# A graph network on one core: one scatter per node row in the first norm, edge rows kept by place, last stage unrolled

## The chip, the cores and the metric

The kernel runs on one core of one Trainium2 chip (trn2). The metric is device time in microseconds (us) of one launch. The engines are TensorE (PE, with its weight loads shown apart as PEld), VectorE (DVE), ScalarE (ACT), GpSimd (POOL) and SyncE (SP). They run their own instruction streams and meet only at semaphores. Plain transfers are issued by SP, indirect ones (a row of a table per partition, by an index) by POOL.

## The reference

`x` is 10000 nodes of 512 floats; there are 5000 edges (`src`, `dst`), sorted by `dst`.

```python
edge_index = jnp.stack([src, dst])
x = _layernorm(x + _L0_gnn_ref(x, W, b, gamma, beta, edge_index), axis=-1)
x = _layernorm(x + _L1_gnn_ref(x, src, dst, edge_attr_20, edge_weight, edge_attr_3, ...), axis=-1)
```

`_L0` is a graph convolution of three layers: each multiplies all rows by a 512x512 weight, adds along every edge the source's row scaled by degrees into the target's row, normalises over all nodes (batch norm) and applies relu. `_L1` takes, for every edge, the row of node `dst` as it comes out of the first layer norm, forms a message with filters made from the edge's attributes, sums the messages of all edges that have the same `src`, and passes the sum through two small weights. A node that is no edge's source gets zero from `_L1`, so its result is only the second layer norm of its row.

## The kernel before, in words

Nodes are laid into 80 tiles. The 40 *edge tiles* (127 nodes each) hold every node that is an edge's target, in the order of the edges sorted by `dst`, with other nodes filled in; the 40 *plain tiles* (123 nodes each) hold the rest. Four tiles make a block, there are 20 blocks, and `kinds` gives their order: two plain, then edge and plain in turn, and two edge blocks at the end. The program is five stages, with a barrier between two of them:

- **order_edges** (L150 to L548), 0 to 176 us. It sorts both ends of the edges with one-hot matmuls and works out where each node lies. Its main loop (L339 to L349 on DVE, L473 to L489 on PE) makes 40 rounds, and in each, for both ends `i`: three small matmuls of `rank`, one of `look` (128x160: counters and 1/sqrt(degree) looked up for 128 keys, L458), one of `new`; on DVE `advance` (L287) and `looks` (L293 and L295, each a product with an accumulated sum). POOL scatters node numbers into `others` (L254, 80 times) beside it.
- **graph_layers** (L551 to L1079), 176 to 1142 us: the three layers, bound by the matmuls of L1020. It leaves the last layer's result in `z`, and each block's own rows in `x_rows`.
- **finish_gcn** (L1082 to L1256) with **EdgePrep** (L1257 to L1435), 1142 to 1398 us. Turn `t` runs from -4 to 19. SP loads `z` and `x_rows` of a block (L1116, L1118). It waits first until block b-3 is turned, then loads `z` of block b, then waits until block b-4 is normalised and loads `x_rows` of b; so the load of `z` for block t+5 is issued after the normalisation of block t. ACT applies the last batch norm to block t+3 (L1218, four instructions), PE transposes block t+2 into PSUM (L1253), DVE adds it to the node's own row and takes mean and variance (L1178, L1183, L1186), four small operations on 128x4 give the factors of both layer norms (L1165 to L1171, L1190), and ACT normalises block t (L1230, four instructions). The second norm of a row that was just normalised needs only one more factor: DVE multiplies by it for two tiles of a block (L1196), ACT for the other two (L1236). POOL then scatters **two** rows per node: the once normalised one into `x2` (L1127), the twice normalised one into the result `out` (L1133); 160 indirect DMAs of 128 rows of 2 KB, all in one queue. EdgePrep is worked into the same turns: at turn 0 DVE reads the sorted edges, waits for all small weights and works out coefficients (`coefficients`, L1343 to L1373); the first layer of the filter network follows at L1311 to L1325, and after the last turn its softplus (ACT L1379, L1398, L1401; DVE L1340). SP issues for it `l_edges` (26 words of each sorted row, L1288), `l_nexti` (one word of each sorted row, 5120 words, L1289) and 13 small weights (L1292).
- **messages** (L1438 to L1612), 1398 to 1643 us: 40 blocks of 128 edges. POOL gathers the rows of `dst` (L1463) and of `src` (L1472), both from `x2`.
- **touched** (L1615 to L1734), 1644 us to the end: softplus of the sums in four parts (ACT L1639, L1642, L1645; DVE L1702, L1706), then 40 blocks in a loop of 8 (`turns`): ACT copies a block for PE (L1652), PE multiplies (L1690), DVE adds, takes statistics and makes the factors (L1721 to L1733), ACT normalises (L1661), POOL copies an index column and scatters (L1675, L1676).

`v.link(...)` is an instruction after which the engine waits for its end before it goes on.

## Time and profile before

| | |
|---|---|
| runs | 1750.26, 1748.43, 1741.68 us; median 1748.43 |
| the profiled execution | 1743.42 us, of which the span of the core is 1741.7 |
| mean granted TensorE clock | 0.870 |
| PE busy | 1375.5 us (79%) |
| DVE busy | 1205.7 us (69%) |
| ACT busy | 948.3 us (54%) |
| POOL busy | 975.6 us (56%) |
| DMA | 340.37 MB, mean 195 GB/s |

Times in the profile are microseconds from the start of the span; a row of a timeline gives start, length, engine, line, operation, result and operands, how many instructions were merged (x4), and in brackets how long the engine had been idle and for what. "issue" means that it waited for nothing that the profile shows.

### The profile page before, as it was taken

Reading aid. Unit: us, or ns where it says so; the run is one execution under the profiler, and the core shown is the slowest. Engines: PE = TensorE matmul, PEld = TensorE weight load, DVE = VectorE, ACT = ScalarE, POOL = GpSimd, SP = SyncE. Lnnn points to the kernel's source line nnn. Section 1 sums busy time; section 2 is a strip of 40 time slices with the busy share of each in tenths; the row PEclk is TensorE's granted clock in tenths of the full one; section 3 lists DMA queues with packets and bytes.
Section 4 is the critical chain, followed back from the end, with each engine's and each line's share of the span. In section 5 each row is a group of like instructions: output and inputs, shape, how many; then the busy total and the mean of one; then the engine's idle time right before and its main releaser. Section 6 shows DMA issues by size and latency. Waiting matters only on the chain. (4 is left out here: it accounts for less than half of the span.)

```text
span 1741.7 us, 27484 instructions
## 1 busy us (share of the span) xinstructions
PE 1375.5 (79%) x8020; PEld 1179.2 (68%) x8020; DVE 1205.7 (69%) x3400; ACT 948.3 (54%) x1906; POOL 975.6 (56%) x986
## 2 busy tenths in 40 slices
PE   4676699999989799999979999935454179999633
PEld 3555488888877688888768888824444068888622
DVE  7247466566665676768667778848777379999765
ACT  3462244334425677767466666428777534444576
POOL 5770667777773687877443333206777644344146
PEclk8589699999999999999989999957566589999955
DMA  2000887878777577777555566279998433323112
GB/s 61 1 2 3 259 301 263 270 256 272 247 239 275 184 253 247 255 255 247 201 185 191 199 210 213 103 227 379 412 398 358 184 92 88 94 84 92 35 75 110
DMA packets 130924, 340.37 MB, mean 195 GB/s; under 512 B 34972, under 2 KB 67220, under 8 KB 127990
## 3 DMA queue, kind: packets, MB, share of 16 engines
q1 hardware_dynamic: 74486, 175.45, 28.6%
q0 software_dynamic: 56320, 163.51, 27.9%
q8 instruction: 55, 0.90, 0.2%
q14 instruction: 63, 0.52, 0.1%
HBM read 166.40 MB, written 177.40 MB: 197 GB/s over the span
## 5 line engine op out<-in xcount | busy, mean ns | idle before, releaser
L1020 PE MATMUL ps_b<-yhi,whi 128*128 128x492 f32 (+1 forms) x960 | 397.1, 414 | 18.9 <-ACT aggT L912 14.3
L1020 PE MATMUL ps_b<-ylo,whi 128*128 128x492 f32 (+1 forms) x960 | 378.2, 394 | 0.0
L1020 PE MATMUL ps_b<-yhi,wlo 128*128 128x492 f32 (+1 forms) x960 | 377.8, 394 | 0.0
L912 ACT COPY aggT<-ps_b 128x492 f32<-128x492 f32 (+1 forms) x240 | 137.6, 574 | 319.8 <-PE ps_b L1020 319.7
L830 DVE BATCH_NORM_STATS2 stat<-aggT 128x6 f32<-128x492 f32 (+1 forms) x240 | 161.9, 676 | 145.6 <-ACT aggT L912 145.4
L672 POOL DMA_INDIRECT rows<-rows_out,node_at x160 | 180.8, 1130 | 110.4 <-ACT rows_out L918 63.3
L1020 PEld LDWEIGHTS ps_b<-yhi,whi 128*128 128x128 f32 x960 | 185.6, 193 | 50.2 <-ACT aggT L912 14.7
L1020 PEld LDWEIGHTS ps_b<-yhi,wlo 128*128 128x128 f32 x960 | 184.0, 192 | 38.1
L1020 PEld LDWEIGHTS ps_b<-ylo,whi 128*128 128x128 f32 x960 | 185.2, 193 | 30.2 <-issue 0.5
L679 POOL TENSOR_TENSOR X<-X,own_row 128x1016 f32<-128x1016 f32 x40 | 96.4, 2412 | 131.5 <-ACT X L896 131.3
L1253 PE MATMUL fin_ps_x<-ident,fin_X 128*123 128x128 f32 (+1 forms) x320 | 69.8, 386 | 102.8 <-DVE fin_xr L1178 73.9
L1253 PEld LDWEIGHTS fin_ps_x<-ident,fin_X 128*123 128x123 f32 (+1 forms) x320 | 61.6, 282 | 117.8 <-DVE fin_xr L1178 78.2
L666 POOL DMA_INDIRECT R<-in_x,node_at x80 | 91.8, 1148 | 87.2 <-DVE R L856 47.2
L760 DVE SCALAR_TENSOR_TENSOR V<-cont,carry,ps_m 128x127 f32<-128x127 bf16 x480 | 132.7, 339 | 6.5 <-PE ps_m L1007 5.3
L1127 POOL DMA_INDIRECT x<-fin_x,node_at x80 | 78.7, 984 | 99.0 <-ACT fin_x L1230 79.2
L782 DVE SCALAR_TENSOR_TENSOR ylo<-X,bn_scale,yhi 128x492 fp32r<-128x492 f32 (+1 forms) x160 | 111.8, 745 | 29.3 <-ACT yhi L881 28.9
L918 ACT COPY rows_out<-ps_c 123x512 f32<-123x512 f32 (+1 forms) x160 | 94.1, 590 | 44.2 <-DMA rows<-rows_out,node_at 44.0
L1031 PEld LDWEIGHTS ps_c<-ident,aggT 128*127 128x127 f32 (+1 forms) x640 | 95.3, 189 | 22.3 <-ACT aggT L912 6.5
L881 ACT ACTIVATE yhi<-X,bn_scale 128x492 fp32r<-128x492 f32 (+1 forms) x160 | 104.4, 710 | 4.2 <-DVE X L773 3.7
L1031 PE MATMUL ps_c<-ident,aggT 128*127 128x128 f32 (+1 forms) x640 | 97.9, 276 | 8.6 <-ACT aggT L912 6.1
L896 ACT ACTIVATE X<-X,bn_shift 128x492 f32<-128x492 f32 (+1 forms) x160 | 103.9, 708 | 0.2 <-DVE bn_scale L733 0.2
L254 POOL DMA_INDIRECT others<-ord_nodeid,ord_place_node x80 | 78.4, 979 | 38.9 <-issue 23.5
(345 smaller groups left out, 3223.5 us busy)
## 6 DMA issues: line engine op xcount, KB each, us to landing
z<-aggT SPq DMA_DIRECT2D x30, 1016.0 KB, 5.1
z<-aggT SPq DMA_DIRECT2D x30, 984.0 KB, 6.1
x_rows<-R SPq DMA_DIRECT2D x80, 256.0 KB, 3.6
fin_xr<-x_rows SPq DMA_DIRECT2D x20, 1024.0 KB, 8.1
X<-z SPq DMA_DIRECT2D x20, 1016.0 KB, 8.1
X<-z SPq DMA_DIRECT2D x20, 984.0 KB, 7.6
fin_X<-z SPq DMA_DIRECT2D x10, 1016.0 KB, 12.6
fin_X<-z SPq DMA_DIRECT2D x10, 984.0 KB, 13.2
```

The lines of the kernel that those rows point to most:

```text
L672: pool.indirect_dma_start(table[layer], bass.IndirectOffsetOnAxis(ap=k.node_at[:, i:i + 1], axis=0), f.rows[j][:], None, bounds_check=m.N ...
L679: nc.gpsimd.tensor_tensor(view, view, k.own_row[:, 4 * o:4 * o + 4, :].rearrange("p t n -> p (t n)") .unsqueeze(1).to_broadcast([P, 2, 4 * ...
L760: nc.vector.scalar_tensor_tensor(f.V[:, j, c, :], k.cont[:, i, 0:EPT], f.carry[i % 2][:, c:c + 1], ps[:, c, 0:EPT], ALU.mult, ALU.add)
L782: nc.vector.scalar_tensor_tensor(f.ylo[g % 2][:, c, 0:n], y, s.scale[:, c:c + 1], hi, ALU.mult, ALU.subtract).then_inc(x["lo"], 1)
L830: nc.vector.bn_stats(k.stat[:, j, 6 * t:6 * t + 6], f.aggT[t % 2][:, j, 0:n]).then_inc(x["counted"], 1)
L881: nc.scalar.activation(f.yhi[g % 2][:, c, 0:n], f.X[g % 3][:, c, 0:n], ACT.Copy, scale=s.scale[:, c:c + 1]).then_inc(x["hi"], 1)
L896: nc.scalar.activation(f.X[g % 3][:, c, 0:n], f.X[g % 3][:, c, 0:n], ACT.Relu, bias=s.shift[:, c:c + 1]).then_inc(x["act_x"], 1)
L912: nc.scalar.copy(f.aggT[t % 2][:, j, 0:cols(t)], f.ps_b[j % 2][:, 0:cols(t)]).then_inc(x["copied"], 1)
L918: nc.scalar.copy(f.rows[j][0:n, :], f.ps_c[j % 2][0:n, :]).then_inc(x["rows"], 1)
L1020: o = nc.tensor.matmul(f.ps_b[j % 2][:, 0:n], w[:, c, j * P:(j + 1) * P], y[g % 2][:, c, 0:n], start=(c == 0 and i == 0), stop=(c == C - 1 ...
L1031: o = nc.tensor.transpose(f.ps_c[j % 2][0:n, c * P:(c + 1) * P], f.aggT[b % 2][:, c, col:col + n], k.ident[:])
L1253: o = nc.tensor.transpose(k.ps_x[j % 2][0:n, c * P:(c + 1) * P], f.X[b % 3][:, c, col:col + n], k.ident[:])
```

## The change

- **order_edges** makes two more facts. For every node a flag says whether it is the source of some edge; it travels beside the node's number (`others` and `node_at` get a second word). For every edge it looks up the *place* of its `dst` row: the last of the equal keys, by a third table of 80 columns in `look` for i = 0 (128x240 there), one more product with a sum per round in `looks`, and a few operations on 128x40. The place is put into the sorted payload in place of `dst`.
- **finish_gcn** scatters one row per node. A node that is a source goes into `out` once normalised, any other twice normalised: the second factor is replaced by 1 through `leaves` and `stays`. For plain blocks both factors are multiplied beforehand, and ACT writes the finished row at once; for edge blocks ACT writes `x2` in SBUF, DVE makes all four result tiles, and SP copies the four whole tiles of 128 lanes into `x2` in DRAM with one plain DMA (`keep`), by place.
- **EdgePrep** at turn 0 waits only for the sorted rows and five small loads; the other eight weights are issued later, and `coefficients` runs at turn 4.
- **messages** gathers the rows of `dst` from `x2` by place and the rows of `src` from `out`; the load of `l_nexti` is issued by SP here.
- **touched** is unrolled: no copies for PE and none of index columns, four PSUM buffers, and square root, reciprocal and shift for four blocks at once.

The core of the diff, each piece moved to the left margin (semaphore lists, shapes of tiles and the indices `node_at[:, i, 0:1]` in place of `node_at[:, i:i + 1]` are left out):

```diff
+nc.gpsimd.tensor_copy(k.payload[:, :, 0], s.key[1][:]).then_inc(packed, 1)
 ge(pool, ranked_nodes, 1)
+ge(pool, flagged, 1)
-                            s.nodeid[:, c:c + 1], None,
+                            s.nodeid[:, c, :], None,
...
+if i == 0:
+    nc.vector.scalar_tensor_tensor(s.junk4[t % 2][:], s.ps_look[i][:, 2 * NC:3 * NC], 1.0, s.hot_col[i][:, t, :],
+                                   ALU.mult, ALU.mult, accum_out=s.tail[:, t:t + 1])
...
+v.link(nc.vector.tensor_scalar(s.flag[:], s.cnt[1][:], 0.0, None, ALU.is_gt))
+nc.vector.tensor_copy(s.nodeid[:, :, 1], s.flag[:]).then_inc(flagged, 1)
+v.link(nc.vector.scalar_tensor_tensor(s.flag[:], s.flag[:], SRC, s.cnt[0][:], ALU.mult, ALU.add))
+v.link(nc.vector.scalar_tensor_tensor(s.flag[:], s.base[0][0][:, 0:NC], -1.0, s.flag[:], ALU.add, ALU.add))
+for table in s.base[0]:
+    nc.vector.tensor_copy(table[:, 2 * NC:3 * NC], s.flag[:]).then_inc(ends, 1)
...
+v.link(nc.vector.tensor_scalar(s.leaves[:], s.tail[:], SRC, None, ALU.is_ge))
+v.link(nc.vector.scalar_tensor_tensor(s.tail[:], s.leaves[:], -SRC, s.tail[:], ALU.mult, ALU.add))
+v.link(nc.vector.scalar_tensor_tensor(s.keyf[1][:], s.leaves[:], MARK, s.keyf[1][:], ALU.mult, ALU.add))
...
+v.link(nc.vector.tensor_scalar(s.tail[:], s.tail[:], float(ET * m.EPT - 1), None, ALU.min))
+v.link(nc.vector.tensor_scalar(s.turnf[:], s.tail[:], 2064.0, 640.0, ALU.mult, ALU.add))
+v.link(nc.vector.tensor_copy(s.turni[:], s.turnf[:]))
+v.link(nc.vector.tensor_scalar(s.tilei[:], s.turni[:], 18, None, ALU.logical_shift_right))
+v.link(nc.vector.tensor_copy(s.turnf[:], s.tilei[:]))
+dve.wait_ge(packed, 5)
+nc.vector.tensor_tensor(k.payload[:, :, 1], s.tail[:], s.turnf[:], ALU.add)
...
+v.link(nc.vector.tensor_scalar(s.leaves[:], s.srt_src[:], MARK, None, ALU.is_ge))
+nc.vector.tensor_copy(k.node_at[:, 0:ET, 1], s.leaves[:]).then_inc(ids, 1)
+v.link(nc.vector.scalar_tensor_tensor(s.srt_src[:], s.leaves[:], -MARK, s.srt_src[:], ALU.mult, ALU.add))
...
-nc.tensor.matmul(s.ps_look[i][:, 0:2 * NC], s.hot_loT[i][:, t * P:(t + 1) * P], s.base[i][t % 2][:],
+wide = s.base[i][0].shape[1]
+nc.tensor.matmul(s.ps_look[i][:, 0:wide], s.hot_loT[i][:, t * P:(t + 1) * P], s.base[i][t % 2][:],
...
+def keep(b):
+    q = m.nth(b) % 2
+    sp.wait_ge(x["normed"], 4 * (b + 1))
+    rows = x2_dram[4 * m.nth(b) * P:4 * (m.nth(b) + 1) * P, :].rearrange("(t p) f -> p t f", p=P)
+    sp.dma_start(rows, f.x2[q][:]).then_inc(kept[q], 16)
...
     sp.dma_start(f.xr[b % 4][:], x_rows[b]).then_inc(x_in[b % 4], 16)
+    if m.edges(b - 4):
+        keep(b - 4)
+    if b == 4:
+        prep.load_late(sp)
+for b in range(NB - 4, NB):
+    if m.edges(b):
+        keep(b)
+for q in range(2):
+    sp.wait_ge(kept[q], 16 * (m.NE // 2))
...
-        pool.wait_ge(x["normed"], n + 1)
-        pool.indirect_dma_start(x2_dram, bass.IndirectOffsetOnAxis(ap=k.node_at[:, i:i + 1], axis=0), f.x2[n % 8][:], None,
-                                bounds_check=m.N - 1, oob_is_err=False).then_inc(put2[n % 8], 16)
-for j in range(4):
-    if runs(t):
-        i, n = m.tile(t, j)[0], 4 * t + j
-        pool.wait_ge(x["edge_out" if j < 2 else "plain_out"], 2 * t + j % 2 + 1)
-        pool.indirect_dma_start(out_dram, bass.IndirectOffsetOnAxis(ap=k.node_at[:, i:i + 1], axis=0), f.out[n % 8][:], None,
+        if m.edges(t):
+            pool.wait_ge(x["made"], 4 * m.nth(t) + j + 1)
+        else:
+            pool.wait_ge(x["normed"], n + 1)
+        pool.indirect_dma_start(out_dram, bass.IndirectOffsetOnAxis(ap=k.node_at[:, i, 0:1], axis=0), f.out[n % 8][:], None,
                                 bounds_check=m.N - 1, oob_is_err=False).then_inc(put[n % 8], 16)
...
-    nc.vector.reciprocal(f.rstd2[q][:], f.std2[q][:]).then_inc(x["ready"], 1)
-if runs(t):
-    for j in range(2):
+    at = slice(m.tile(b, 0)[0], m.tile(b, 0)[0] + 4)
+    v.link(nc.vector.reciprocal(f.rstd2[q][:], f.std2[q][:]))
+    v.link(nc.vector.tensor_tensor(f.rstd2[q][:], f.rstd2[q][:], f.stays[:, at], ALU.mult))
+    nc.vector.tensor_tensor(f.rstd2[q][:], f.rstd2[q][:], f.leaves[:, at], ALU.add).then_inc(x["ready"], 1)
+    if m.plain(b):
+        dve.wait_ge(x["ready"], b + m.nth(b) + 1)
+        v.link(nc.vector.tensor_tensor(f.nmr[q][:], f.nmr[q][:], f.rstd2[q][:], ALU.mult))
+        nc.vector.tensor_tensor(f.rstd[q][:], f.rstd[q][:], f.rstd2[q][:], ALU.mult).then_inc(x["ready"], 1)
+if m.edges(t):
+    for j in range(4):
         n = 4 * t + j
         dve.wait_ge(x["normed"], n + 1)
         ge(dve, put[n % 8], 16 * (n // 8))
-        nc.vector.tensor_scalar(f.out[n % 8][:], f.x2[n % 8][:], f.rstd2[t % 2][:, j:j + 1], None,
-                                ALU.mult).then_inc(x["edge_out"], 1)
+        nc.vector.tensor_scalar(f.out[n % 8][:], f.x2[m.nth(t) % 2][:, j, :], f.rstd2[t % 2][:, j:j + 1], None,
+                                ALU.mult).then_inc(x["made"], 1)
...
+act.wait_ge(x["ready"], t + 1 + m.nth(t) + 1 if m.plain(t) else t + 1 + m.kinds[:t].count("P"))
+if m.edges(t):
+    ge(act, kept[e % 2], 16 * (e // 2))
+    ge(act, x["made"], 4 * (e - 1))
 for j in range(4):
     n = 4 * t + j
-    ge(act, put2[n % 8], 16 * (n // 8))
-    nc.scalar.activation(f.x2[n % 8][:], f.xr[t % 4][:, j, :], ACT.Identity,
+    if m.plain(t):
+        ge(act, put[n % 8], 16 * (n // 8))
+    dst = f.x2[e % 2][:, j, :] if m.edges(t) else f.out[n % 8][:]
+    nc.scalar.activation(dst, f.xr[t % 4][:, j, :], ACT.Identity,
                          scale=f.rstd[q][:, j:j + 1], bias=f.nmr[q][:, j:j + 1]).then_inc(x["normed"], 1)
-for j in range(2, 4):
-    n = 4 * t + j
-    ge(act, put[n % 8], 16 * (n // 8))
-    act.wait_ge(x["normed"], n + 1)
-    nc.scalar.activation(f.out[n % 8][:], f.x2[n % 8][:], ACT.Copy,
-                         scale=f.rstd2[q][:, j:j + 1]).then_inc(x["plain_out"], 1)
...
-if t == 0:
+if t == 4:
     prep.tensor_first(pe)
...
+self.loads = [(l.bf1[:], w["bf1"].rearrange("(f o) -> f o", o=1))]
 self.loads += [(l.Wf1[32 * g:32 * g + self.nbr, g, :], w["Wf1"]) for g in range(4)]
+self.late = [(l.Ws[:], w["W_in2f_s"]), (l.Wv[:], w["W_in2f_v"]), (l.W2s[:], w["W2_s"]), (l.W2v[:], w["W2_v"]),
+             (l.W1s[:], w["W1_s"].rearrange("(f c) o -> f c o", c=2)),
+             (l.W1v[:], w["W1_v"].rearrange("(f c) o -> f c o", c=2)),
+             (l.Wf2[:], w["Wf2"][:, 0:4 * P]),
+             (l.bf2[:], w["bf2"][0:4 * P].rearrange("(o f) -> o f", o=1).to_broadcast([P, 4 * P]))]
...
-sp.dma_start(l.nexti[:], self.sorted[1:m.EPAD + 1, :].rearrange("(t p) w -> p t w", p=P)[:, :, 0]).then_inc(s["nexts"], 16)
...
+def weighs(self, t):
+    return t.s == 4
...
         if not t.runs(0):
             return
@@ -1340,23 +1400,26 @@
             nc.vector.scalar_tensor_tensor(l.hT[:, part], l.big[:, part], -LOG2, l.hT[:, part], ALU.add, ALU.add).then_inc(s["made"], 1)
...
+def first(self, dve):
+    m, nc, l, s = self.m, self.m.nc, self.l, self.s
     v = Steps(dve, s["own"])
     dve.wait_ge(s["rows"], 16)
-    dve.wait_ge(s["nexts"], 16)
-    for dst, src in ((l.skey, l.edges[:, :, 0]), (l.next, l.nexti[:])):
-        v.link(nc.vector.tensor_copy(dst[:], src))
-    for dst, src in ((l.src, l.edges[:, :, 0]), (l.dst, l.edges[:, :, 1])):
-        v.link(nc.vector.tensor_scalar(dst[:], src, m.N - 1, None, ALU.min))
+    v.link(nc.vector.tensor_copy(l.skey[:], l.edges[:, :, 0]))
+    v.link(nc.vector.tensor_scalar(l.src[:], l.edges[:, :, 0], m.N - 1, None, ALU.min))
+    v.link(nc.vector.tensor_copy(l.end[:], l.edges[:, :, 1]))
     v.link(nc.vector.memset(l.rows[:, 0:4], -1.0))
     for q in range(2):
         v.link(nc.vector.memset(l.fst[q][:], 0.0))
+    dve.wait_ge(s["loaded"], 16 * len(self.loads))
+    self.steps = v
...
+@block.sync
+def _(sp):
+    with nc.allow_non_contiguous_dma(reason="one word of each sorted row"):
+        sp.dma_start(l.nexti[:], by_src[1:m.EPAD + 1, :].rearrange("(t p) w -> p t w", p=P)[:, :, 0]).then_inc(s["nexts"], 16)
...
-pool.indirect_dma_start(own[r], None, x2_dram,
+pool.indirect_dma_start(own[r], None, out_dram,
...
+dve.wait_ge(s["nexts"], 16)
+nc.vector.tensor_copy(l.next[:], l.nexti[:]).then_inc(s["none"], 1)
+dve.wait_ge(s["none"], 2)
...
+def root(g):
+    act.wait_ge(s["aggr"], GS * (g + 1))
+    nc.scalar.activation(l.std[:, group[g]], l.mv[:, group[g], 1], ACT.Sqrt, bias=k.eps[:, 0:1]).then_inc(s["root"], 1)
+root(0)
+for g in range(NG):
+    if g + 1 < NG:
+        root(g + 1)
+    act.wait_ge(s["nmr"], g + 1)
+    for b in range(GS * g, GS * g + GS):
+        ge(act, put[b % RING], 16 * (b // RING))
+        nc.scalar.activation(l.Y[b % RING], l.X[:, b, :], ACT.Identity,
+                             scale=l.rstd[:, b:b + 1], bias=l.nmr[:, b:b + 1]).then_inc(s["done"], 1)
...
+for b in range(ET):
+    ge(pool, s["done"], b + 1)
+    pool.indirect_dma_start(out_dram, bass.IndirectOffsetOnAxis(ap=l.row[:, b:b + 1], axis=0), l.Y[b % RING], None,
+                            bounds_check=m.N - 1, oob_is_err=False).then_inc(put[b % RING], 16)
...
+for b in range(ET):
+    pe.wait_ge(s["plus"], b // per + 1)
+    ge(pe, s["ysum"], b - 3)
+    nc.tensor.matmul(l.ps[b % 4][:, 0:P], l.sT[:, P * b:P * (b + 1)], l.W2s[:], start=True, stop=True).then_inc(s["prod"], 1)
...
+def scales(g):
+    dve.wait_ge(s["root"], g + 1)
+    nc.vector.reciprocal(l.rstd[:, group[g]], l.std[:, group[g]]).then_inc(s["rec"], 1)
+    dve.wait_ge(s["rec"], g + 1)
+    nc.vector.scalar_tensor_tensor(l.nmr[:, group[g]], l.mv[:, group[g], 0], -1.0, l.rstd[:, group[g]],
+                                   ALU.mult, ALU.mult).then_inc(s["nmr"], 1)
+for i in range(parts):
+    plus(i)
+for b in range(-2, ET):
+    if b + 2 < ET:
+        dve.wait_ge(s["prod"], b + 3)
+        nc.vector.tensor_tensor(l.X[:, b + 2, 0:P], l.X[:, b + 2, 0:P], l.ps[(b + 2) % 4][:, 0:P], ALU.add).then_inc(s["ysum"], 1)
+    if 0 <= b + 1 < ET:
         dve.wait_ge(s["ysum"], b + 2)
-    if t.runs(0):
+        ge(dve, s["aggr"], b)
+        nc.vector.bn_stats(l.st[(b + 1) % 2][:], l.X[:, b + 1, :]).then_inc(s["stats"], 1)
+    if b >= 0:
         dve.wait_ge(s["stats"], b + 1)
-        ge(dve, s["aggr"], b)
+        nc.vector.bn_aggr(l.mv[:, b, :], l.st[b % 2][:]).then_inc(s["aggr"], 1)
+        if b % GS == 1 and b >= GS:
+            scales(b // GS - 1)
+scales(NG - 1)
...
-x2_dram = m.dram("x2", [n_nodes, d])
+x2_dram = m.dram("x2", [EPAD, d])
...
-a.others = m.dram("others", [m.NPAD, 1], I32)
+a.others = m.dram("others", [m.NPAD, 2], I32)
...
-k.node_at = m.sb("node_at", [P, 2 * ET], I32)
+k.node_at = m.sb("node_at", [P, 2 * ET, 2], I32)
```

## Rows read from the trace of the kernel before

**Rows 1.** Stretches: us, busy us (xcount) of PE, PEld, DVE, ACT, POOL, PEclk, DMA share, GB/s.

```profile
1200.00:1320.00 120.00, 59.77 (x256) 50.16 (x257) 91.68 (x252) 94.56 (x156) 91.64 (x94) 0.63 1.01 407
...
1425.00:1643.00 218.00, 215.68 (x1694) 191.94 (x1692) 207.37 (x694) 92.86 (x289) 79.77 (x135) 1.00 0.29 83
...
1670.00:1742.00 72.00, 27.55 (x70) 17.26 (x70) 43.17 (x185) 48.20 (x111) 46.43 (x78) 0.50 0.29 112
```

**Rows 2.** Timeline, POOL: first and last scatter of finish_gcn, start of the next stage.

```profile
1181.05 1.03 POOL L1127 DMA_INDIRECT x<-fin_x,node_at  x1 [74.90 <-ACT fin_x L1230]
...
1388.48 0.97 POOL L1133 DMA_INDIRECT out<-fin_out,node_at  x1 [0.31 <-issue]
...
1397.59 0.18 POOL L1474 COPY l_idx<-l_dst 128x1 int32<-128x1 int32 x1 [8.14 <-SPq L1453]
```

**Rows 3.** Loads of finish_gcn: landing times, KB each, and ACT's wait.

```profile
DMA to landing us min/median/max: 5.2/12.6/14.7
...
fin_xr<-x_rows SPq DMA_DIRECT2D x20, 1024.0 KB, 8.1
...
ACT fin_X L1218 <- DMA fin_X<-z: 28.2, 11, 6.5
```

**Rows 4.** Timeline, DVE and ACT in two turns of finish_gcn.

```profile
1240.20 0.68 DVE L1317 TENSOR_TENSOR l_diag<-ident,l_skey 128x512 f32<-128x512 f32 x1
...
1241.90 2.90 ACT L1218 ACTIVATE fin_X<-fin_X,bn_shift,bn_scale 128x508 f32<-128x508 f32 x4
1242.03 0.18 DVE L1165 RECIPROCAL fin_rstd<-fin_std 128x4 f32<-128x4 f32 x1 [1.14 <-ACT fin_std L1213]
1242.24 0.16 DVE L1167 SCALAR_TENSOR_TENSOR fin_nmr<-fin_mv,fin_rstd 128x4 f32<-128x4 f32 x1
...
1244.89 2.92 ACT L1230 ACTIVATE fin_x<-fin_xr,fin_nmr,fin_rstd 128x512 f32<-128x512 f32 x4
...
1250.84 0.18 DVE L1165 RECIPROCAL fin_rstd<-fin_std 128x4 f32<-128x4 f32 x1 [0.84 <-ACT fin_std L1213]
...
1259.70 0.68 DVE L1317 TENSOR_TENSOR l_diag<-ident,l_skey 128x512 f32<-128x512 f32 x1
```

**Rows 5.** Timeline, SP and DVE around turn 0, and the start of turn 18.

```profile
1146.65 15.54 SPq L1289 DMA_DIRECT2D l_nexti<-by_src  x1
...
1165.88 0.14 DVE L1190 RECIPROCAL fin_rstd<-fin_std 128x4 f32<-128x4 f32 x1
...
1173.04 0.23 DVE L1362 TENSOR_SCALAR l_Ws<-l_Ws 128x128 f32<-128x128 f32 x1 [3.52 <-DMA l_Wf<-in_L_gnn_Wf]
...
1178.00 0.20 DVE L1311 COPY l_fst<-l_edges 128x80 f32<-128x80 f32 x1
...
1353.08 0.19 DVE L1311 COPY l_fst<-l_edges 128x80 f32<-128x80 f32 x1
```

**Rows 6.** Timeline, ACT and DVE: softplus behind the last turn.

```profile
1370.38 0.67 ACT L1379 ACTIVATE l_big<-fin_ps_c,l_bf 128x512 f32<-128x512 f32 x1
...
1380.35 5.70 DVE L1340 SCALAR_TENSOR_TENSOR l_hT<-l_big,l_hT 128x1280 f32<-128x1280 f32 x4 [8.53 <-ACT l_big L1401]
```

**Rows 7.** order_edges: lines L458 and L293, duration ns min/median/max, first and last start.

```profile
L458 PE MATMUL ord_ps_look<-ord_base,sel x80: 299/364/607, 32.7 to 145.6; 128*128 128x160 f32 x80
...
L293 DVE SCALAR_TENSOR_TENSOR ord_junk<-ord_ps_look,ord_hot_col x80: 231/233/241, 33.8 to 146.5; 128x80 f32<-128x80 f32 x80
```

**Rows 8.** touched: one block on DVE, softplus' end, the last scatter of the chain.

```profile
1657.90 5.70 DVE L1706 SCALAR_TENSOR_TENSOR l_sT<-l_rows,l_sT 128x1280 f32<-128x1280 f32 x4 [7.98 <-ACT l_rows L1645]
...
1687.27 0.29 DVE L1721 TENSOR_TENSOR l_X<-l_X,l_ps 128x128 f32 x1 [0.33 <-PE l_ps L1690]
1687.48 0.69 DVE L1723 BATCH_NORM_STATS2 l_st<-l_X 128x6 f32 x1
1688.08 0.16 DVE L1726 BATCH_NORM_AGGREGATE l_mv<-l_st 128x2 f32<-128x6 f32 x1
...
1735.16 0.97 POOL out L1676
```

162 lines of the change are left out of this document (55 added, 107 removed).

## The prediction, made before the changed kernel was run

> **What bounds the kernel now.** I read the table by stretches first. In finish_gcn PE works half of the time, DVE 91.7, ACT 94.6 and POOL 91.6 of 120 us, and the DMA engines show 1.01 at 407 GB/s; in messages PE is busy 215.7 of 218 us; in touched no engine reaches two thirds [rows 1]. So the parts touched differ in kind. POOL's timeline tells who is last in finish_gcn: its 160 scatters run from 1181.05 to 1388.48, one per (1388.48-1181.05)/159 = 1.30 us of which 0.97 is the instruction, without a pause, and the next stage starts at 1397.59, 9.1 us after the start of the last one [rows 2]. POOL is the tail. But it is not alone: 18 turns, from turn 0 (1178.00) to turn 18 (1353.08), take 9.73 us each [rows 5], while eight scatters take 10.4. The turns run a little ahead and POOL falls behind, as far as its buffers let it. A second loop holds the turns at nearly the same pace: the load of z for block t+5 is issued after the norms of block t and is wanted before those of t+2, so two turns hold a landing of 12.6 us (median), four relus 2.9, four norms 2.9 and some 1.2 of issue and root: 19.6, or 9.8 a turn; ACT waits 28.2 us in all for z [rows 3, 4]. Third comes DVE: 1240.20 to 1259.70 is two turns, 19.5 us, of which 0.84 and 1.14 are waits for ACT's root; that leaves 8.76, with a little waiting for norms in it, so a turn that waits for nobody costs DVE 8.7 [rows 4].
>
> In touched the last link is POOL's scatter at 1735.16, but it follows a DVE, ACT, PE round: a block's own work on DVE is 0.21, 0.60 and 0.09 (distances of starts), and the wait for PE alone adds 0.33 [rows 8].
>
> **The sum, part by part**, against the profiled execution's 1743.4 (median of the runs 5.0 above it, lowest 1.7 below).
>
> *order_edges.* The 40 rounds alternate between PE and DVE, ACT in places. Each gets a third table: 80 more columns on a 160-column matmul of 0.30 (shortest), so up to 0.15 on PE, and a product of 0.23 with its read, so up to 0.31 on DVE [rows 7]. Nothing, if both fall into waits, up to 0.46 x 40 = 18. I take 0.16 a round, the nearer value since the new product follows its like without a wait and PE's part lies partly beside it: +6.4. Behind the loop come three linked operations of some 0.2 (the step from L1165 to L1167, [rows 4]), +0.6; the five before the sorted result arrives lie in DVE's wait for PE, uncovered they cost 1.2; three behind it run beside SP's two broadcast loads. The flags and two table copies before the loop fill DVE's wait for ACT's root; without it, 1.2. POOL's 80 scatters of two words instead of one start half a microsecond later and end well before the loop. **+7**, ends +1 and +20.
>
> *graph_layers.* 40 gathers of two words for one, the same number of packets, in a stage held by PE: 0.
>
> *finish_gcn, start.* DVE has nothing of turn -1 left at 1165.88 but starts turn 0 at 1178.00: it waits for l_nexti, whose issue alone holds SP for 15.54, and then for weights queued behind it until 1173.04, and works out the coefficients [rows 5]. After, the three factors of the mix add 0.8, `first` costs 1.3, and turn 0 starts at 1168.0 if l_edges has landed, 10.0 earlier. The coefficients come back at turn 4, (1178.00-1173.04) + 0.6 for the squares, with 0.4 for a busier PE: +6.0. The two casts of flags at the top stand in DVE's wait before the first z. l_edges keeps its place ahead of the small loads, so the load of block 3 may go as late as before; ACT has one turn of slack for it.
>
> *finish_gcn, turns.* POOL issues 4 per turn, 5.2 us, and drops out. ACT loses two of its six passes of 0.7. DVE keeps two result tiles per turn on average (four in edge turns, none in plain ones) and gains two links of 0.2 each turn and two more in plain ones: 8.7 + 0.6 = 9.3. The z loop: half of POOL's traffic is gone, but every second turn SP puts the copy of 1 MB of x2 ahead of z. If the plain queue gets 300 of 407 GB/s instead of 200 (half of the rate, as its half of the bytes now), 2 MB take 7 us and 3 MB 10, plus the 2 of an idle landing: 9 to 12 and the 7.0 above give 8.0 to 9.5 a turn. I take **9.3**: 18 x (9.73-9.3) = -7.7. The bytes allow it: 407 x 9.73 = 3.96 MB a turn, less 1.05 scattered and plus 0.52 copied is 3.43, 8.4 us at 407 GB/s.
>
> The Trainium skill (DMA: Bandwidth & Descriptors, Specifications) speaks against part of this: it puts HBM's share of one core at about 358 GB/s. This trace moved 407 for 120 us [rows 1], so the measurement decides; by the page the turn would be 3.43/0.358 = 9.6 and the whole 5 us longer.
>
> *finish_gcn, tail.* From turn 18 to the next stage is 1397.59-1353.08 = 44.5 us, and POOL's backlog is its end [rows 2, 5]. Without it the end is ACT's: 1.7 us of factors and root, then the norms of blocks 18 and 19 at 2.9 each [rows 4], end 7.5 us after the start of turn 18; then the softplus chain, which ran from 1370.38 to 1386.05, 15.7 [rows 6], and 1.2 of barrier (an estimate; of the 8.1 in front of the next stage [rows 2] I count the rest to the last landing): 24.4. POOL's last four scatters and the last copy land before that. -20.1. So finish_gcn: -10.0 + 6.0 - 7.7 - 20.1 = **-31.8**.
>
> *messages.* PE bound [rows 1]; where the gathered rows lie costs nothing in transfers that are 3 blocks ahead. l_nexti now runs beside the first gathers. Bounds: 0, and the 15.54 of its issue if the gathers stood behind it. They are in another queue; I take 1, plus 0.3 for the copy at the end: **+1.3**.
>
> *touched.* The softplus chain stays, DVE is free at 1663.60. Then a block costs 0.21+0.60+0.09 = 0.9, since no operation waits for the one before it, and PE runs up to four blocks ahead. ACT's first row waits for block 7's moments (its second root stands ahead of it): 1.0 to fill, 8 x 0.9, one pair of scales 0.35: 1672.1. Root, shift and 0.8 of row: POOL starts at 1673.3. DVE and ACT (3.2 per four blocks) are now faster than POOL's 1.30 a scatter [rows 2], so POOL is the end: 1673.3 + 39 x 1.30 = 1724.0 against 1735.16: **-11.2**. PE at its low clock has 27.55/40 = 0.7 a block and hides [rows 1].
>
> Sum: 7 - 31.8 + 1.3 - 11.2 = -34.7, 1743.4 - 34.7 = **1708.7**.
>
> **Rivals.**
>
> (a) *The turns do not shorten.* DVE's waits for ACT and the landings stay, 9.73 holds: +7.7, 1716. For it: DMA share 1.01, z's landing already twice a load's idle time. Against: a queue half gone. With the dear end of order_edges 1727.
>
> (b) *Slower.* The x2 copy stands ahead of z in SP's one queue, and that queue keeps its present rate: the landing in every second turn grows by 3/2 to 18.9, the turn to (18.9+7.0)/2 = 13.0, and the total to 1708.7 + 18 x 3.7 = 1775. It decides from a landing of 15.4 (a turn of 11.2) on. For it: a 14.7 exists already [rows 3]. Against: eight scatters of the other queue compete today, four then.
>
> (c) *Faster.* l_edges lands early, a lighter DMA shortens waits, order_edges hides its table (-6), turns of 8.7: -10.8. 1692 to 1698.
>
> (d) *touched does not move*: if the unrolled loop still hands each block around, the -11.2 is missing, 1720. Nothing in the new order of waits asks for it.
>
> **How the numbers follow.** Forecast 0.56, (a) 0.20, (c) 0.12, (d) 0.08, (b) 0.04. The range goes from (c)'s low end 1691 to (a) with the dear table 1727. A measurement of this kernel can tell about 0.5%, 8.7 us, from no change: under 1734.7 lie all but (b) and mishaps added up, faster 0.93, same 0.03, slower 0.04.
>
> **What would show it.** Right: POOL idle about half of the time in finish_gcn; turn 0 near 1175 in the new clock (7 later from order_edges, 10 earlier here); turns near 9.3 with DVE rarely waiting; messages starting 17 to 19 after the end of the last norm; POOL in touched in steps of 1.3 without gaps. Wrong: order_edges longer by over 12, ACT waiting for z in most turns (a, b), a first gather of messages that lands after 10 us, or DVE steps in touched over 1.3.

## The result, and the profile after

The changed kernel takes 1728.25 us (median of 5 runs, 1726.16 to 1731.84) against 1741.68 (1738.87 to 1750.26) before: ratio 0.9923, 95% interval 0.9897 to 0.9948. The forecast was 1708.7, with a range of 1691 to 1727. The sign was right, and the time missed the range by 1.3 us. The profiled execution took 1726.16 us with a span of 1724.5, 17.2 less than the span before, where the sum had said 34.7.

The page of the changed kernel, the busy time of each engine and three rows of the 40 slices (43 us each):

```profile
span 1724.5 us, 26873 instructions
...
PE 1368.7 (79%) x8020; PEld 1171.3 (68%) x8020; DVE 1213.7 (70%) x3500; ACT 905.4 (53%) x1796; POOL 889.3 (52%) x865
...
POOL 5770567777774678777552343302333533433226
...
DMA  2000697777867676777664566448998733333113
GB/s 62 2 2 2 220 315 253 256 257 253 271 226 261 209 246 246 249 258 258 222 202 158 202 206 207 151 186 290 337 343 326 302 85 91 85 93 90 55 45 142
```

POOL lost 86 us of work and is 2 to 5 tenths busy in finish_gcn (slices 28 to 32). From 1200 to 1320 the transfers fell from 407 GB/s [rows 1] to 327: fewer bytes, but not in less time.

The timeline of DVE, the first instruction of each stretch: end of the 40 rounds, graph_layers, its last statistics, turn 0, the coefficients at turn 4 and the instruction behind them, turn 18, messages, touched.

```profile
149.57 0.43 DVE L365 TENSOR_TENSOR ord_pos<-ord_pos,ord_rank 128x40 f32<-128x40 f32 x2
...
180.04 4.27 DVE L884 MEMSET R<- 128x512 f32 x8 [1.56 <-PEq L101]
...
1144.83 0.69 DVE L858 BATCH_NORM_STATS2 stat<-aggT 128x6 f32<-128x508 f32 x1 [2.09 <-ACT aggT L940]
...
1175.69 0.20 DVE L1371 COPY l_fst<-l_edges 128x80 f32<-128x80 f32 x1
...
1214.01 0.28 DVE L1420 TENSOR_TENSOR l_yv<-l_edges 128x120 f32<-128x120 f32 x1
...
1219.47 0.20 DVE L1371 COPY l_fst<-l_edges 128x80 f32<-128x80 f32 x1
...
1364.69 0.20 DVE L1371 COPY l_fst<-l_edges 128x80 f32<-128x80 f32 x1
...
1390.54 0.91 DVE L1679 MEMSET l_agg<- 128x1024 f32 x1 [1.58 <-PEq L101]
...
1638.48 0.20 DVE L1749 TENSOR_TENSOR l_more<-l_skey,l_next 128x40 f32<-128x40 f32 x1 [1.25 <-PEq L101]
```

The same marks in each kernel give a table of stages; each column is one profiled execution, in us between marks, and sums to its span. Three columns are experiments told below, run on one chip. Changed by: the second column less the first.

| stretch | before | changed | changed by | forecast | z first (e12) | copy twice (e13) | before, new last stage (e14) |
|---|---|---|---|---|---|---|---|
| order_edges | 176.4 | 180.0 | +3.6 | +7 | 181.1 | 179.8 | 174.6 |
| graph_layers, to its last statistics | 960.8 | 964.8 | +4.0 | 0 | 959.3 | 968.5 | 957.5 |
| to turn 0 | 40.8 | 30.9 | -9.9 | -10.0 | 31.0 | 30.8 | 41.2 |
| turn 0 to turn 18, coefficients within | 175.1 | 189.0 | +13.9 | +6.0 - 7.7 | 162.8 | 213.8 | 174.5 |
| turn 18 to messages | 44.8 | 25.8 | -19.0 | -20.1 | 25.8 | 27.8 | 46.1 |
| messages | 246.5 | 247.9 | +1.4 | +1.3 | 248.2 | 248.0 | 246.8 |
| touched, to the end | 97.4 | 86.0 | -11.4 | -11.2 | 86.0 | 86.0 | 86.0 |

Four of the seven rows are within 1.1 us of the forecast, order_edges came out 3.4 cheaper and graph_layers 4.0 dearer, and one row holds the miss: the turns, 15.6. Without the coefficients (1219.47 - 1214.01 = 5.5) 18 turns take 183.5, 10.2 each, where 9.73 [rows 5] had been and 9.3 was forecast. Both are means over turns of unlike length: in the kernel before, two turns take 15.9, 16.6 and 19.2 up to turn 6 and 20.6 on average from there on; in the changed kernel they take 21.2 from turn 6 on, 0.7 more. Of the 8.4 that the 18 turns grew by, 4.5 lie ahead of turn 6: turns 2 and 3 take 22.2 without the coefficients, for 16.6, and there z is asked for behind the norms and the eight late weights.

Who waits in them is in the table of waits from 1150 to 1380 (us in total, times, longest), ACT, DVE and POOL:

```profile
ACT fin_X L1267 <- DMA fin_X<-z: 56.1, 13, 7.4
...
DVE fin_rstd L1233 <- ACT fin_std L1272: 20.6, 8, 4.1
...
POOL out L1176 <- DVE fin_out L1245: 94.9, 16, 14.0
```

ACT waits for z twice as long as before [rows 3]; DVE waits, once in each edge turn, for the root that ACT takes behind z's relu; POOL waits for all of them. The timeline of SP, ACT and POOL shows one round of it, two turns long:

```profile
1262.57 2.86 ACT L1267 ACTIVATE fin_X<-fin_X,bn_shift,bn_scale 128x492 f32<-128x492 f32 x4 [5.70 <-DMA fin_X<-z]
...
1265.52 2.92 ACT L1284 ACTIVATE fin_x<-fin_xr,fin_nmr,fin_rstd 128x512 f32<-128x512 f32 x4
...
1267.81 0.97 POOL L1176 DMA_INDIRECT out<-fin_out,node_at  x1 [9.51 <-DVE fin_out L1245]
...
1268.46 0.32 SPq L1155 DMA_DIRECT2D fin_xr<-x_rows  x1
1268.83 0.43 SPq L1149 DMA_DIRECT2D x<-fin_x  x1
1269.30 0.64 SPq L1153 DMA_DIRECT2D fin_X<-z  x1
...
1277.26 0.97 POOL L1176 DMA_INDIRECT out<-fin_out,node_at  x1 [0.31 <-issue]
...
1284.09 2.86 ACT L1267 ACTIVATE fin_X<-fin_X,bn_shift,bn_scale 128x492 f32<-128x492 f32 x4 [6.36 <-DMA fin_X<-z]
```

The four norms of an edge block end at 1268.4. Only then SP issues x_rows, the copy of x2 and z, in this order; z's relu starts at 1284.09, 14.8 after z's issue, and the round begins again 21.5 after it began (1284.09 - 1262.57). In the first ten of them POOL issues eight scatters, those of the edge block and of the plain block behind it, one per 1.28 but for a wait of 0.8. The DMA view from 1200 to 1360 gives the landings (KB each, median us), and the second block is the rate in 40 slices of 1.07 us from 1257 to 1300:

```profile
fin_xr<-x_rows SPq DMA_DIRECT2D x14, 1024.0 KB, 8.7
x<-fin_x SPq DMA_DIRECT2D x8, 1024.0 KB, 11.1
fin_X<-z SPq DMA_DIRECT2D x7, 1016.0 KB, 14.1
fin_X<-z SPq DMA_DIRECT2D x6, 984.0 KB, 14.6
```

```profile
GB/s 391 390 403 432 440 413 430 430 405 250 8 122 61 362 408 398 402 417 425 384 413 413 392 440 428 432 437 408 378 15 0 91 107 377 429 337 429 398 421 420
```

The three transfers land one after the other, 8.7, 11.1, 14.1: a queue. (The 8.7 is the median over both kinds of turns; the x_rows that goes first in a round lands in 6.1.) The rate is 360 to 440 for 17 us and then falls to near nothing for 3 to 4: in each round the DMA engines run dry, because the next loads are asked for only after the norms that the last z held up.

touched did what was forecast. POOL's timeline there, first, second and last scatter:

```profile
1667.99 1.00 POOL L1734 DMA_INDIRECT out<-l_msg,l_row  x1 [42.44 <-ACT l_msg L1726]
1669.30 1.00 POOL L1734 DMA_INDIRECT out<-l_msg,l_row  x1 [0.30 <-ACT l_msg L1726]
...
1717.89 0.97 POOL L1734 DMA_INDIRECT out<-l_agg,l_row  x1 [0.31 <-issue]
```

That is (1717.89 - 1667.99)/39 = 1.28 each, without a gap, and the last one starts 79.4 after the stage's first DVE instruction, against 90.8 before (1735.16 [rows 8] less 1644.33, the start of that stage's first DVE instruction).

### The profile page after: what moved, and what is told of

It reads as the page before. It is cut to its first block and busy times, and to the rows that moved or that the text cites. A ratio compares the mean times of both kernels' runs of the same rounds, so it can differ in the third digit from the quotient of the medians.

```text
span 1724.5 us, 26873 instructions
## 1 busy us (share of the span) xinstructions
PE 1368.7 (79%) x8020; PEld 1171.3 (68%) x8020; DVE 1213.7 (70%) x3500; ACT 905.4 (53%) x1796; POOL 889.3 (52%) x865
## 5 line engine op out<-in xcount | busy, mean ns | idle before, releaser
L1048 PE MATMUL ps_b<-yhi,whi 128*128 128x492 f32 (+1 forms) x960 | 398.5, 415 | 19.7 <-ACT aggT L940 15.1
L700 POOL DMA_INDIRECT rows<-rows_out,node_at x160 | 187.3, 1170 | 108.9 <-ACT rows_out L946 60.9
L1176 POOL DMA_INDIRECT out<-fin_out,node_at x80 | 79.2, 991 | 185.1 <-DVE fin_out L1245 94.9
L788 DVE SCALAR_TENSOR_TENSOR V<-cont,carry,ps_m 128x127 f32<-128x127 bf16 x480 | 132.8, 340 | 12.2 <-PE ps_m L1035 11.2
L1059 PE MATMUL ps_c<-ident,aggT 128*127 128x128 f32 (+1 forms) x640 | 97.5, 276 | 9.0 <-ACT aggT L940 6.1
L1035 PE MATMUL ps_m<-sel,G 128*128 128x128 f32 x640 | 87.1, 281 | 15.9 <-DMA G<-in_x,srci 15.8
## 6 DMA issues: line engine op xcount, KB each, us to landing
fin_X<-z SPq DMA_DIRECT2D x10, 1016.0 KB, 14.1
```

The source lines that it names most:

```text
L700: pool.indirect_dma_start(table[layer], bass.IndirectOffsetOnAxis(ap=k.node_at[:, i, 0:1], axis=0), f.rows[j][:], None, bounds_check=m.N - ...
L788: nc.vector.scalar_tensor_tensor(f.V[:, j, c, :], k.cont[:, i, 0:EPT], f.carry[i % 2][:, c:c + 1], ps[:, c, 0:EPT], ALU.mult, ALU.add)
L1048: o = nc.tensor.matmul(f.ps_b[j % 2][:, 0:n], w[:, c, j * P:(j + 1) * P], y[g % 2][:, c, 0:n], start=(c == 0 and i == 0), stop=(c == C - 1 ...
L1059: o = nc.tensor.transpose(f.ps_c[j % 2][0:n, c * P:(c + 1) * P], f.aggT[b % 2][:, c, col:col + n], k.ident[:])
```

## The experiments

The theory is the **z loop**: the turns are held by a round of z's landing, relu and norms, and what the change added to it is the megabyte of copy put ahead of z, which is asked for late. The rivals are **bytes** (the transfers need that time in any order) and **links** (DVE's new linked operations).

**Two kinds of chips.** e1 to e11 and e16 fell on chips on which the kernel before takes 1919 to 1944 us; e12 to e15 on one where it takes 1740.56, as in the forecast's own table. What differs is seen in e9, the kernel before on the former kind: its POOL timeline has sixteen scatters in regular steps of 1.28 and then two that start 8.3 apart. The second block is DVE in front of that gap, the third the same kind of wait in touched (e8), and the fourth is from e1, a wait in order_edges (us, times, longest) that is 1.9 at the longest in the changed kernel's first trace:

```profile
1439.08 0.97 POOL L1127 DMA_INDIRECT x<-fin_x,node_at  x1 [0.30 <-issue]
1447.34 0.97 POOL L1133 DMA_INDIRECT out<-fin_out,node_at  x1 [7.29 <-DVE fin_out L1196]
```

```profile
1435.53 0.69 DVE L1178 TENSOR_TENSOR fin_xr<-fin_xr,fin_ps_x 127x512 f32<-127x512 f32 x1 [5.28 <-DMA ord_raw<-in_edge_attr]
1441.84 1.43 DVE L1178 TENSOR_TENSOR fin_xr<-fin_xr,fin_ps_x 127x512 f32<-127x512 f32 x2 [5.62 <-DMA ord_raw<-in_edge_attr]
```

```profile
1873.36 0.16 DVE L1693 SCALAR_TENSOR_TENSOR l_nmr<-l_mv,l_rstd 128x4 f32<-128x4 f32 x1 [3.90 <-DMA R<-in_L_gnn_W]
```

```profile
PEld ord_ps_t L458 <- ACT sel L545: 67.9, 8, 55.4
```

POOL's gap ends when DVE has made the next `fin_out`: POOL has nothing to scatter, its queue does not stop. DVE itself stands twice before, 5.28 and 5.62 us, at the sum of L1178, and the profile puts both waits to a DMA of the first stage, so it does not name what they are for; PE's transposes for the tile added at 1435.53 are recorded as done at 1429.0. In e8 DVE waits 3.90 for its own reciprocal of L1691, one instruction earlier. So on these chips engines stand for several us for results that the trace has as made, and in the first stages for tens of us several at a time (in e1 PE 55, DVE 39, ACT 30); what causes it stays open. In finish_gcn the kernel before has such a gap in every two turns, which are 16 scatters; the changed kernel has hardly any (1.0 us in e5 from turn 6 on). Totals are therefore compared within one kind only; the turns of the changed kernel are the same on both (e5 below). The expectations of e9, e12, e14 and e16 speak of pauses or stops in POOL's queue: so I read these gaps then.

**e1, z first.** The loop over b is shifted by one, so that SP asks for z as soon as block b-3 is turned:

```diff
-for b in range(3, NB):
-    sp.wait_ge(x["turned"], 4 * (b - 2))
-    sp.dma_start(f.X[b % 3][:, :, 0:cols(b)], z_in[b, :, :, 0:cols(b)]).then_inc(z_got[b % 3], 16)
-    ge(sp, x["normed"], 4 * (b - 3))
-    sp.dma_start(f.xr[b % 4][:], x_rows[b]).then_inc(x_in[b % 4], 16)
-    if m.edges(b - 4):
-        keep(b - 4)
-    if b == 4:
-        prep.load_late(sp)
+for b in range(3, NB + 1):
+    if b < NB:
+        sp.wait_ge(x["turned"], 4 * (b - 2))
+        sp.dma_start(f.X[b % 3][:, :, 0:cols(b)], z_in[b, :, :, 0:cols(b)]).then_inc(z_got[b % 3], 16)
+    r = 3 if b == 3 else b - 1
+    if b != 4:
+        ge(sp, x["normed"], 4 * (r - 3))
+        sp.dma_start(f.xr[r % 4][:], x_rows[r]).then_inc(x_in[r % 4], 16)
+        if m.edges(r - 4):
+            keep(r - 4)
+        if r == 4:
+            prep.load_late(sp)
```

> The changed kernel, but in finish_gcn SP issues the load of z for block t+5 as soon as block t+2 is turned, ahead of x_rows of block t+4 and of the copy of block t, which wait for the norms of block t. Theory (z loop): in the changed kernel 18 turns take 10.2 us each (without the coefficients) because z is asked for only after the norms of an edge block, behind 1 MB of x_rows and 1 MB of copy, lands 14 us later, and ACT waits for it in every edge turn; DVE without that wait needs 18.47 for two turns (20.95 - 2.48, and 22.56 - 4.12 alike). So 9 x (20.4 - 18.5) = 17 less than the changed kernel's 1728: 1711, ratio to before 0.982. Rival (bytes): the DMA engines are the limit whatever the order, two turns move 7.2 MB; the order changes nothing, 1728. Rival (links): the new linked operations of DVE hold the turns; 1728 as well, and ACT's wait for z would vanish while the turns stay.

**e2, the copy behind z.** z still waits for the norms.

```diff
 sp.dma_start(f.X[b % 3][:, :, 0:cols(b)], z_in[b, :, :, 0:cols(b)]).then_inc(z_got[b % 3], 16)
+if m.edges(b - 5):
+    keep(b - 5)
 ge(sp, x["normed"], 4 * (b - 3))
 sp.dma_start(f.xr[b % 4][:], x_rows[b]).then_inc(x_in[b % 4], 16)
-if m.edges(b - 4):
-    keep(b - 4)
...
-for b in range(NB - 4, NB):
+for b in range(NB - 5, NB):
```

> The changed kernel, but SP issues the copy of an edge block behind the load of z that followed it; z still waits for the norms, behind x_rows. It separates the two things that hold z in the z loop: the megabyte of copy ahead of it (2.5 us at 415 GB/s) and the time at which it is asked for. If the copy ahead is what lengthened the turns: 2.5 of the 3.1 that DVE waits in an edge turn go, 9 x 2.5 = 22, at most down to DVE's 18.5 for two turns, so 1711 to 1713. If the time of asking is what counts and the transfers share the rate anyway: 0 to 5 less, 1723 to 1728. Bytes: 1728.

**e3, no copy** (the first hunk is SP's in finish_gcn, the second in order_edges; the waits for the copies are left out too, and the result is not the reference's).

```diff
-sp.dma_start(rows, f.x2[q][:]).then_inc(kept[q], 16)
...
+for r in range(10):
+    sp.dma_start(a.x2[4 * P * r:4 * P * (r + 1), :], a.x[4 * P * r:4 * P * (r + 1), :]).then_inc(x2_made, 16)
```

> The changed kernel with the ten copies of edge blocks left out of finish_gcn: x2 is filled in the first stage from x, where the DMA engines are idle, so messages gathers other rows of the same size, and the result is not the reference's. Theory (z loop): z loses 1 MB ahead of it and the engines 1.05 MB of 7.2 in two turns; turns fall to DVE's 18.5 for two, 1711. Bytes: 6.2 of 7.2 MB leave 20.4 x 0.86 = 17.5, below DVE's need, so also 1711: this run shows the copy's whole price and says with the copy behind z whether its place or its bytes cost. Links: 1728.

**e4, four buffers for z.** All other `b % 3` of finish_gcn become `b % 4`, and the last turn asks for no z.

```diff
-f.X = [m.sb(f"fin_X{i}", [P, C, m.COLS]) for i in range(3)]
+f.X = [m.sb(f"fin_X{i}", [P, C, m.COLS]) for i in range(4)]
...
+sp.dma_start(f.X[3][:, :, 0:cols(3)], z_in[3, :, :, 0:cols(3)]).then_inc(z_got[3], 16)
...
-    sp.dma_start(f.X[b % 3][:, :, 0:cols(b)], z_in[b, :, :, 0:cols(b)]).then_inc(z_got[b % 3], 16)
+    sp.dma_start(f.X[(b + 1) % 4][:, :, 0:cols(b + 1)], z_in[b + 1, :, :, 0:cols(b + 1)]).then_inc(z_got[(b + 1) % 4], 16)
```

> The changed kernel with four buffers for z instead of three: SP's order stays (x_rows, copy, z, all behind the norms), but the z that it loads there is that of block t+6, one turn further ahead. Theory (z loop): a landing of 14 then spans three turns instead of two, ACT never waits for z, and turns fall to DVE's 18.5 for two: 1711. Bytes or links: 1728.

Measured: 1845.22, 1843.73, 1828.77 and 1841.43 us beside 1943.68 of before. No changed kernel ran beside them on that chip, so the turns decide, and e5 below is their control. From turn 6 on, two turns take 17.5 to 18.1 in all four (17.79 to 17.86 in e1, 17.5 to 18.1 in e2, 17.5 to 17.8 in e3, 17.8 to 17.9 in e4), and DVE waits for ACT's root 0.4 in all from there on instead of 1.0 to 4.1 per edge turn. Bytes and links are out: in e1, e2 and e4 the same bytes move, and the same links run, in 8.9 a turn. That moving the copy alone is enough (e2) puts the cost on the copy's place in the queue, not on its bytes; asking for z earlier is enough as well (e1, e4). The two differ in turns 2 and 3, with the coefficients within: 23.7 and 23.6 in e1 and e4, 27.7 and 28.0 in e2 and e3, 27.7 in the changed kernel. That part belongs to the late asking and not to the copy. e3's lower total is not the turns' (168.9 from turn 0 to 18, 164.8 in e1); its order_edges is 265.4 long, in the other three 282.0 to 284.0. ACT's waits from 1360 to 1480 in e2 tell how near it still is; in e1 the same line is absent:

```profile
ACT fin_X L1267 <- DMA fin_X<-z: 14.7, 5, 3.8
```

**e5, the changed kernel as control, and e6, z first beside it.**

> The changed kernel itself, beside the two that follow and the kernel before, on one chip: the four runs so far were on a chip where the kernel before takes 1943.7 and stands still for tens of microseconds in the first two stages, so their totals can't be set against 1728. Their finish_gcn can: 17.8 for two turns in each of the four. If the z loop is a matter of the kernel and not of the chip, this run shows some 20.5 for two turns and DVE waiting for ACT's root in the edge turns wherever it runs; if that other chip simply runs the turns at 17.8, this run would show it there too, and the four runs would prove nothing.

> The first experiment once more (z ahead of x_rows and the copy), beside the changed kernel. z loop: 17.8 for two turns as on the other chip, so 9 x (20.4 - 17.8) = 23 less than the changed kernel, some 1705 where that one is at 1728. Bytes or links: equal to it.

Measured: e5 1865.15 (ratio to before 0.9623, 0.9584 to 0.9661), e6 1844.86 (0.9506, 0.9469 to 0.9543). e5's pairs of turns from turn 6 are 20.6, 21.1, 21.6, 22.8, 22.0, 20.8, those of the first trace 19.5, 21.0, 21.5, 22.6, 21.9, 21.0: the loop belongs to the kernel. z first takes 20.3 off.

**e7, z first, two of an edge block's four results made by ACT**: DVE's loop becomes `for j in range(2)`, and on ACT, behind the norms:

```diff
+for j in range(2, 4) if m.edges(t) else ():
+    n = 4 * t + j
+    ge(act, put[n % 8], 16 * (n // 8))
+    act.wait_ge(x["normed"], n + 1)
+    nc.scalar.activation(f.out[n % 8][:], f.x2[e % 2][:, j, :], ACT.Copy,
+                         scale=f.rstd2[q][:, j:j + 1]).then_inc(x["made2"], 1)
```

> z first, and of an edge block's four result tiles ACT makes two and DVE two, as in the kernel before (ACT is busy 86 of 120, DVE 106). If DVE holds the turns once z comes in time: an edge turn loses 2 x 0.4 on DVE, 17.0 for two turns, 9 x 0.8 = 7 less than z first. If the transfers are next (7.2 MB at the 374 to 384 GB/s of those turns is 18.8 to 19.3, at the 415 of the fullest slices 17.4): no or little gain, 0 to 4, and ACT waits for z again.

Measured: 1845.93 (0.9531, 0.949 to 0.9572), the same as e6. But the turns are not: 19.0 to 20.1 for two from turn 6 on, from turn 0 to 18 175.3 against 164.3 in e6. In the two profiled executions a graph_layers shorter by 11.4 takes up the difference; whether it does so in the others no run shows. No z is waited for, so the transfers are not next. From turn 6 on DVE waits 19.7 where it adds x_rows (L1224), 8.7 in e6, and 6.9 of them are put to the same DMA of the first stage as the standstills of e9. So the work lifted from DVE did not shorten the turn; whether another engine's part grew or this chip's standstills came in is not settled.

**e8, the kernel before with the new touched** (the function, and its tiles for moments and scales, as in the change; the edit is that part of the change's diff).

> The kernel before with only touched taken from the changed kernel. The prediction put 11.2 on it, the changed kernel's own trace shows its last scatter 79.4 after the stage's first DVE instruction, against 90.9 before: 11.4. Alone it should give the same, ratio 0.9935. Rival: part of it came from what lies ahead (the clock, l_nexti, an emptier queue) and the part alone gives less than 8.

Measured: 1934.61 beside 1939.17 (0.9975, 0.994 to 1.0009), which doesn't tell it from no change. touched is 91.5 long there and 97.5 in e9: 6.0 of the 11.4, under the 8 of the rival. It has two gaps in POOL of 4.0 from start to start, and 2 x (4.0 - 1.28) = 5.4 is what it takes longer than 86.0. The old stage takes 97.5 in e9, as on the other chip (97.4), and has no gap in POOL; whether it met no standstill or had slack for it is not shown.

**e9, the kernel before itself.**

> The kernel before itself, for its profile beside the others of this call, so that stages can be set against each other on one chip. If this is again the chip on which the kernel before takes 1939: my theory is that its 74 of gain there (0.9623) comes from finish_gcn, because the scatters there come with pauses of 5 to 8 us in POOL's queue and the kernel before has 160 of them in that stage against 80; so turns of 14.1 each, as in the kernel before with the new last stage (28.3 for two), against the changed kernel's 10.4, and touched longer than 91.4 by some 5 to 11. Rival: the gain is in the first two stages (the standstills of tens of us), which the change touches little: then order_edges is longer here than 281.

Measured: 1924.25 (1.0017, 0.9985 to 1.0049). Against e5: turns 240.2 and 190.7, tail 35.3 and 26.5, touched 97.5 and 91.8, order_edges 274.8 and 281.0. Two turns take 27.4 to 29.0 from turn 4 on: 16 scatters at 1.28 and one gap come to 15 x 1.28 + 8.26 = 27.5. The gain there, 3.8%, comes from finish_gcn as expected, and the rival (the first stages) is out. The reason given for it, pauses in POOL's queue, is not: POOL waits for DVE in each gap, and DVE stands 81.7 us in all at L1178. Why these standstills come in finish_gcn with the kernel before and not with the changed one is not shown.

**e10, the kernel before with z first** (the edit of e1 without the copy), and **e16**, once more:

> The kernel before with only SP's order changed (z ahead of x_rows). In the kernel before I read POOL's 160 scatters as the tail of finish_gcn: a load that comes earlier then lets ACT and DVE run ahead, but POOL's last scatter and the end of the stage stay: 0 to 3 less, ratio 0.998 to 1.0. Rival: the z loop held the kernel before too (9.73 a turn against POOL's 10.4 for eight scatters), and it gains 10 or more.

> The kernel before with only SP's order changed (z ahead of x_rows), again. On a chip without stops: the turns of before take 9.73, the z loop's own pace is 9.8 by the prediction's reading and POOL's is 10.2 for eight scatters. If POOL is the tail: turns may run ahead a little at first, then POOL's buffers hold them, POOL's last scatter stays, total 0 to 4 less (ratio 0.998 to 1.0). If the z loop held the stage: 10 or more less.

Measured: 1.0002 (0.9965 to 1.0039) and 0.999 (0.996 to 1.002), pairs of turns mostly 28 as in e9. That they gain nothing says little of z: on these chips hardly anything waits for it (in e9 ACT's long wait is the one for DVE's moments, 12 at the longest), the standstills hold the turns, and POOL waits too. For the chip of the forecast the trace of before says more: POOL scatters from 1181.05 to 1388.48 without a gap [rows 2], so an earlier z could not have ended the stage sooner. From turn 6 on its two turns take 20.6, its 16 scatters 20.9, and z's round, with a landing of 13.2 there, 20.2: the two loops were even, and which one held a given turn stays open.

**e11, no third product** (`tail` is set to 0 behind the loop).

```diff
-if i == 0:
-    nc.vector.scalar_tensor_tensor(s.junk4[t % 2][:], s.ps_look[i][:, 2 * NC:3 * NC], 1.0, s.hot_col[i][:, t, :],
-                                   ALU.mult, ALU.mult, accum_out=s.tail[:, t:t + 1])
```

> The changed kernel without the third product of the 40 rounds of order_edges (the place of dst; it is left out, so messages gathers other rows and no row counts as a source; the wider matmul stays). I had put 0.16 on a round for it, 6.4; the changed kernel's loop ends only 2.75 later than before. If DVE's waits for PE took in most of it: the loop ends 1 to 3 earlier than the changed kernel's. If the 2.75 is PE's wider matmul alone: 0 to 0.5.

Measured: 1851.26 (0.9645, 0.9598 to 0.9693). The loop ends at 247.0; in six executions of kernels with the product on such chips it ends at 250.6 to 253.5, in four of the kernel before, without the whole table, at 241.0 to 246.5. That points to 3.6 or more for the product, somewhat over the 1 to 3 expected. But a seventh with the product, e3, ends at 234.9: its standstills fell otherwise (one of 68 us on DVE where e1 has four of 15 to 39), and these move the mark by more than the product does. So the size is not shown.

**e12, z first, e15, the changed kernel, e14, the new touched alone, and e13, the copy twice**, all on the chip without standstills. e13 (`more` is the same rows of a further tensor):

```diff
 sp.dma_start(rows, f.x2[q][:]).then_inc(kept[q], 16)
+sp.dma_start(more, f.x2[q][:]).then_inc(kept[q], 16)
```

> z first, a third time, beside the changed kernel (e15). On a chip without stops in POOL's queue: 9 x (20.4 - 17.8) = 23 less than the changed kernel, 1705, ratio to before 0.979. On a chip with them: 20 less, as in e6. If the gain there came from the stops and not from the z loop, it is under 5 on a chip without them.

> The changed kernel, but SP issues each copy of an edge block twice, the second into a further tensor that nobody reads, both ahead of z. z loop by the prediction's formula, two turns = landing + 7.0: landing 14.3 plus 1.05 MB at 415 GB/s (2.5) gives 16.8 + 7.0 = 23.8 for two turns against 21.3, and 9 x 2.5 = 23 more in all. If the copy had not been in z's way, or if the landing were set by something other than bytes: pairs as in the changed kernel (20.5 to 22.8) and a total within 5 of it.

> The kernel before with only the new touched, again. On a chip without stops: touched 86.0 long as in the changed kernel's trace, 97.4 before, so 11.4 less. With stops after every 16 scatters (two more waits of 3): 91.5 against 97.5, 6 less.

> The changed kernel as the companion of e12 to e14 on their chip. Without stops 0.992 of before; with them 0.962 as in e5.

| | median us | ratio to before (1740.56) | 95% |
|---|---|---|---|
| e12 z first | 1700.67 | 0.9775 | 0.9745 to 0.9804 |
| e15 changed | 1726.21 | 0.9912 | 0.9886 to 0.9938 |
| e14 new touched alone | 1727.92 | 0.9916 | 0.9892 to 0.994 |
| e13 copy twice | 1757.16 | 1.0094 | 1.0067 to 1.012 |

z first takes 25.5 off the changed kernel (23 expected) and beats both kernels. Its round in SP's timeline, then z's landings from 1230 to 1370 and the busy times of one stretch (columns as in [rows 1]):

```profile
1266.58 0.53 SPq L1154 DMA_DIRECT2D fin_X<-z  x1
1269.58 0.32 SPq L1158 DMA_DIRECT2D fin_xr<-x_rows  x1
1269.95 0.43 SPq L1149 DMA_DIRECT2D x<-fin_x  x1
1277.38 0.32 SPq L1154 DMA_DIRECT2D fin_X<-z  x1
1277.80 1.00 SPq L1158 DMA_DIRECT2D fin_xr<-x_rows  x1
1284.09 0.53 SPq L1154 DMA_DIRECT2D fin_X<-z  x1
```

```profile
DMA to landing us min/median/max: 8.5/9.4/10.2
```

```profile
1207.00:1327.00 120.00, 57.89 (x289) 48.23 (x289) 107.04 (x326) 87.56 (x144) 50.96 (x50) 0.74 0.99 388
```

z is asked for 3 us ahead of x_rows and the copy and lands in 9.4; the round is 1284.09 - 1266.58 = 17.5, DVE is busy 107 of 120, and the DMA engines move 388 GB/s with a share of 0.99, so they hardly run dry. In e13 z lands in 17.4 (1230 to 1380) and DVE's wait for ACT's root doubles:

```profile
DMA to landing us min/median/max: 14.6/17.4/18.0
```

```profile
DVE fin_rstd L1235 <- ACT fin_std L1274: 43.8, 8, 6.8
```

Two turns take 25.1 (24.7 to 25.5), where the formula, landing + 7.0, gives 24.4: the landing grew by 3.1, not by the 2.5 that one megabyte takes at the full rate. With 14.3 the formula gives 21.3 for the changed kernel, whose pairs average 21.2. The total grew by 31 (23 expected). The turns are 24.8 of them and the tail 2.0, by the table and e15's stages; the rest is not placed. e14 gives touched its 86.0 and 12.6 in the total.

## Why the prediction was wrong

**The step that failed** is the landing in the term of the turns: "If the plain queue gets 300 of 407 GB/s instead of 200 (half of the rate, as its half of the bytes now), 2 MB take 7 us and 3 MB 10, plus the 2 of an idle landing: 9 to 12". It was 14.3. The formula around it, two turns = landing + 7.0, held at both sizes, within 0.1 and 0.7. DVE's own need was forecast at 9.3 a turn and is 8.8 with z first, where DVE waits only 7.3 of 105 us, all for PE; that e3 takes the same with a megabyte less says that bytes don't hold it. I had spread the scatters evenly, four to a turn. They come in a bunch: with z late, the plain turn follows the edge turn at once, and eight scatters, 2.1 MB, run just while x_rows, the copy and z, 3.1 MB, are in flight. The bytes by queue (q1 plain, q0 POOL's) within one landing of z, 1248.36 to 1262.54 in the changed kernel, and then one in the kernel before, 1240.71 to 1253.93:

```profile
q1 hardware_dynamic: 1258, 3.58, 72.7%
q0 software_dynamic: 504, 1.66, 28.7%
```

```profile
q1 hardware_dynamic: 760, 2.76, 52.4%
q0 software_dynamic: 840, 2.72, 50.7%
```

So the plain queue got 3.58 MB in 14.2 us, 252 GB/s, not 300, against 209 before. Over the whole stage half of the scatters had gone, but within z's landing their bytes fell only from 2.6 to 2.8 MB to 1.5 to 2.1, while the plain bytes rose. The 2 of an idle landing is about right: the copy issued at 1355.37, alone in its queue beside 0.52 MB of scatters, lands in 5.05. Of the 17.5 us by which the sum was off, the turns are 16. The prediction's pace of 9.73 for the kernel before hides a part of this: it is a mean with the short turns at the start, and from turn 6 on a turn took 10.3. One of its own signs of being wrong came true: ACT waits for z, 13 times and 56.1 us in all.

**The rivals.** (b) named the mechanism, the copy ahead of z in SP's one queue, at 4%, but priced it at 18.9 (the rate of before) and 1775, slower. (a) had its effect, ACT still waiting, with turns of 9.73 at 1716. The truth lay between a landing of 12 and one of 15.4, where I had no case: the two rivals and the forecast were three prices of one quantity and should have been one range, 9 to 18.9, from which the turns follow. The end of the range, 1727, came from (a) with a dear table in order_edges; that the measured time lies so near to it is luck, for order_edges was cheap and the turns dearer than (a).

**order_edges**, +3.6 of 7: the round's DVE wait for PE took in a good part of the third product. The loop ends 2.75 later (149.57 against 146.82), and e11 points to the product for it. The mark has a spread of its own: on the chip of e12 to e15 it lies at 145.0 without the table and at 149.3, 150.6 and, for the changed kernel itself (e15), 156.3 with it. The five operations before the sorted result cost nothing, as forecast.

**graph_layers**, +4.0 of 0: nothing in that stage changed but the index's second word. Over all profiled executions on chips without standstills it took 957.5 and 960.8 with the code of before and 959.3, 964.8, 966.2, 968.5 with the new; z first, with the same code as the others, is among the lowest. I put this down to the spread of the stage, which is not proof.

**Start of finish_gcn** -9.9 (-10.0), **coefficients** +5.5 (+6.0), **messages** +1.4 (+1.3) and **touched** -11.4 (-11.2, alone 12.6 in the total) were right, each by its own steps. **The tail** was 1.4 longer than forecast (25.8 of 24.4). POOL's last scatter starts at 1377.14, while the softplus chain runs from 1372.13 to 1388.96 and messages starts at 1390.54: with half of the scatters gone, the softplus chain is the end. It took 16.8 where 15.7 was forecast.

**Weighed rule.** The prediction set HBM's share of one core, about 358 GB/s by the Trainium skill (DMA: Bandwidth & Descriptors, Specifications), against the 407 of [rows 1]. z first moved 388 over 120 us, and the full slices above reach 440, so the measurement stands; the lower rates of the changed kernel are engines that ran dry.

**Where the expected gain went**: not to contention as such, for the bytes fit (e1 moves them in 8.9 a turn), but to a round that was there before and into which the change put a further megabyte. The version that takes the wait out moves one load ahead of one wait, and it ends up below the forecast, at 1700.67.

## What to carry to other kernels

When a transfer is added to a queue, look at what stands behind it and whether that is on a round that closes on itself; there its full length counts in each round (2.5 forecast and 3.1 measured for the second megabyte in e13), whatever the averages of bytes allow. Issue a load when its buffer comes free, not behind waits that belong to its neighbours in the program. And price a landing by the bytes in flight in its own window, with the bursts as they are issued, not by mean rates.

## What the runs showed of the hardware that I had not expected

- Chips differ. The kernel before took 1919 to 1944 on three chips and 1740 on another. On the three, engines stand still: for up to 68 us in the first stages, for 5 to 8 at a time in every two turns of finish_gcn with the kernel before, for some 4 in the new touched (e8). The cause is open. The change's worth goes from 0.9% to 3.8% with it.
- Large transfers of the plain queue land in the order in which they were issued, in every round that was read, each behind the bytes ahead of it: x_rows 8.7, copy 11.1, z 14.1, with one more megabyte 17.4. They are not strictly one at a time: within z's landing above 3.58 MB moved, more than the 3.1 of x_rows, copy and z, so the next x_rows was already under way.
- A chain of scatters of 128 rows of 2 KB goes at one per 1.28 to 1.30 us, 0.97 of it the instruction, in finish_gcn and in touched alike.
